# Loads of stage two issued from one queue, and the stage-one transpose in two instructions

## What is computed

```
adj = relu(einsum('bn,tnm->btm', x.reshape(b, n*d), masker_param) + masker_bias)   # b, t, 50, 50
adj = adj / (adj.sum(-1) + 1e-6)
m = einsum('btnm,btmd->btnd', adj, x @ weight)
r, z, ng = split(m @ w_ih.T + b_ih + x @ w_hh.T + b_hh, 3)
h = (1 - sigmoid(z)) * tanh(sigmoid(r) * ng) + sigmoid(z) * x
h = layernorm(batchnorm(h)); w = softmax(h @ attn_w.T + attn_b); out = einsum('btn,btnd->btd', w, h)
```

## Time and profile before

| what | value |
| --- | --- |
| median of 3 runs | 2257.29 us (2251.59 to 2257.75) |
| time of the profiled execution | 2254.87 us |
| its span, first to last instruction | 2253.1 us |
| PE busy | 2141.4 us (95%) |
| DVE, ACT, POOL busy | 1221.3, 866.1, 66.7 us |
| granted TensorE clock, mean | 0.971 |
| q1 (SP) and q10 (ACT) moved | 237.53 MB and 37.69 MB |

### The profile page before, as it was taken

How to read it: one execution, slowest core, us unless ns; L and a number is a source line. 1 busy time by engine, 2 the same in 40 slices (tenths; PEclk the granted TensorE clock), 3 DMA queues, 4 the chain that set the end, 5 groups by cost and what they waited for, 6 DMA issues and landing times. The chain is left out here.

```text
span 2253.1 us, 33249 instructions
## 1 busy us (share of the span) xinstructions
PE 2141.4 (95%) x11694; PEld 1680.5 (75%) x11694; DVE 1221.3 (54%) x2370; ACT 866.1 (38%) x1471; POOL 66.7 (3%) x68
## 2 busy tenths in 40 slices
PE   8999999999999999999999999998988988996898
PEld 7888888888888888888888887776766766775333
DVE  5444334444265443344443453776776766878667
ACT  4211111111033111111110123776876776875862
POOL 0000000000000000000000000100100110110000
PEclk9999999999999999999999999998999998998899
DMA  7321222221254212222202234675556566564660
GB/s 249 140 100 51 93 99 104 99 95 45 104 187 147 105 56 83 99 104 102 101 35 104 104 103 119 160 171 162 150 153 167 137 158 171 141 177 138 196 184 11
DMA packets 148058, 276.08 MB, mean 123 GB/s; under 512 B 11565, under 2 KB 106061, under 8 KB 143053
## 3 DMA queue, kind: packets, MB, share of 16 engines
q1 hardware_dynamic: 129836, 237.53, 34.7%
q10 hardware_dynamic: 18144, 37.69, 5.6%
HBM read 196.01 MB, written 79.17 MB: 122 GB/s over the span
## 5 line engine op out<-in xcount | busy, mean ns | idle before, releaser
L431 PE MATMUL psum<-w_hi,x_lo 128*128 128x500 f32 x2080 | 806.3, 388 | 8.2 <-DVE w_lo L289 8.2
L431 PE MATMUL psum<-w_lo,x_hi 128*128 128x500 f32 (+1 forms) x2080 | 807.8, 388 | 0.0
L431 PE MATMUL psum<-w_hi,x_hi 128*128 128x500 f32 x1920 | 743.2, 387 | 0.0
L340 DVE TENSOR_REDUCE rows<-u 128x10 f32<-128x500 f32 x160 | 107.7, 673 | 741.4 <-ACT u L302 741.3
L302 ACT ACTIVATE u<-psum 128x500 f32<-128x500 f32 x160 | 93.9, 587 | 1048.0 <-PE psum L431 1048.0
L431 PEld LDWEIGHTS psum<-w_hi,x_lo 128*128 128x128 f32 x2080 | 391.0, 188 | 88.8 <-issue 8.2
L431 PEld LDWEIGHTS psum<-w_lo,x_hi 128*128 128x128 f32 (+1 forms) x2080 | 390.8, 188 | 78.1
L431 PEld LDWEIGHTS psum<-w_hi,x_hi 128*128 128x128 f32 x1920 | 360.6, 188 | 72.3
L746 PE MATMUL psum<-adj_sb,xs_sb 100*64 100x100 f32 x2048 | 222.6, 375 | 4.4 <-PEq L148 4.4
L746 PEld LDWEIGHTS psum<-adj_sb,xs_sb 100*64 100x64 f32 x2048 | 154.7, 153 | 55.8 <-issue 39.4
L609 ACT ACTIVATE r_gate<-psum,bias 64x400 f32<-64x400 f32 x256 | 151.2, 591 | 60.5 <-PE psum L773 58.9
(11 more groups left out here) (168 smaller groups left out, 2103.9 us busy)
## 6 DMA issues: line engine op xcount, KB each, us to landing
w_raw<-W SPq DMA_DIRECT2D x140, 500.0 KB, 6.5
adjT<-at SPq DMA_DIRECT2D x160, 320.0 KB, 2.3
adj_sb<-adjT SPq DMA_DIRECT2D x32, 800.0 KB
xs_sb<-xz SPq DMA_DIRECT2D x16, 1600.0 KB
hF<-hC ACTq DMA_DIRECT2D x96, 256.0 KB, 2.9
h<-hF SPq DMA_DIRECT2D x64, 256.0 KB, 4.0
adj_sb<-adjT SPq DMA_DIRECT2D x32, 450.0 KB
xg_sb<-xg ACTq DMA_DIRECT2D x14, 800.0 KB, 17.3
```

The costliest lines, as they stand in the source:

```text
L340: nc.vector.tensor_reduce(rows[:, 0], u[:, c2], AX.X, ALU.add).then_inc(dve_step, 1)
L431: last = nc.tensor.matmul(mm_out(w % 2), a[0:r, w, k, :], b[0:r, k, :], start=k == 0 and n == 0, stop=k == KF and n == 1)
```

## The change

SP now issues all three loads of stage two. Its wait per tile is for `h_ready` (the last state of tile t) in place of `ax_done`, and `load_xg` stands ahead of `load_adj` and `load_xs`. `reload_xg` leaves ACT. In stage one `turn_squares` issues two transposes of 320 columns in place of one of 640; only the second signals.

```diff
--- before.py
+++ after.py
@@ -355,7 +355,8 @@
                     dve.wait_ge(an_cleared, 1)
                 else:
                     dve.wait_ge(at_stored[c2], 8 * (c - c2))
-                nc.vector.transpose(at[:, c2], an[:].rearrange("p n (k s) -> p k n s", s=TB)).then_inc(at_ready, 1)
+                nc.vector.transpose(at[:, c2, 0], an[:, :, 0:TB])
+                nc.vector.transpose(at[:, c2, 1], an[:, :, TB:2 * TB]).then_inc(at_ready, 1)
 
             def weight_blocks(dve):
 
@@ -533,7 +534,8 @@
                 for r in range(2):
                     tile = it * 2 + r
                     if more:
-                        sp.wait_ge(ax_done, (tile + 1) * ROUNDS)
+                        sp.wait_ge(h_ready, (tile + 1) * ROUNDS)
+                        load_xg(sp, shared, ins, tile + 2, r)
                         load_adj(sp, shared, adjT, tile + 2, r)
                         load_xs(sp, shared, ins, tile + 2, r)
 
@@ -559,11 +561,6 @@
         @block.scalar
         def _(act):
             act.wait_ge(bias_ready, 1)
-
-            def reload_xg(tile, r):
-
-                act.wait_ge(h_ready, (tile - 1) * ROUNDS)
-                load_xg(nc.scalar, shared, ins, tile, r)
 
             def x_hi(it, r, k):
 
@@ -619,8 +616,6 @@
                     nc.scalar.activation(n_bank(s), n_in[:, s % 2], ACT.Tanh).then_inc(n_ready, 1)
                     if q and (r or not (isinstance(it, int) and it == 0)):
                         store(it * 2 + r - 1, q - 1)
-                    if q == 0 and (r and more or not r and not (isinstance(it, int) and it == 0)):
-                        reload_xg(it * 2 + r + 1, 1 - r)
 
             nc.scalar.activation(r_gate[:, 0:1], bias[:, 0:1], ACT.Sigmoid).then_inc(warmed, 1)
             for k in range(XPARTS):
```

## The result

The changed kernel takes 2263.66 us (median of 20 runs) against 2255.35 us for the kernel before (20 runs beside it): a ratio of 1.0039, 95% interval 1.0030 to 1.0048. It is slower by 0.4%, some 9 us. The profiled execution of after took 2261.48 us, its span is 2259.5, its mean granted clock 0.972.

The account below looks back on a forecast made before the run. Stage one was taken as PE-bound, stage two as bound by no engine alone, with waits. Later loads (+34.3 us) and transposes (+0.2) made +34.5 on 2254.9: 2289 us, 1.4% slower, range 2275 to 2315.

Parts of the forecast that it names:

- The mechanism: Stage two: loads start 10.7 us later and land 7.2 us after PE gets there; PE waits in tiles 1 to 14.
- The length of the loads: Stage two, tiles 1 to 14: loads need 32.7 us, landing 32.8 us after the last state.
- the sign that this step is wrong: Stage two: SP's issue to PE's release under 31 or over 35 us would show the load step wrong.
- The other way to the number: Loads read from the middle of stage two: about 28 us, with xg_sb ahead 28.0 to 33.3; not the one taken.
- Were it all of the 800 KB, they would add nothing: Stage two: if q10's old stretch already held all of xg_sb, moving it ahead adds 0 us, otherwise up to 5.3.
- The release: Stage two: from PE's release to the tile's last state 12.2 us, taken from tile 0; at least 10.7 by tile 5.
- DVE's stop: DVE's 38.8 us in 5 stops at L644, after stage two's jump back; 48 more instructions can end or keep it.
- the forecast hardly hangs on it: Stage two: if DVE's stop stays, five tiles take 45.7 us, +3.5 us in all; if it goes, 45.0 holds.
- Rival 1: Stage two: loads of 30.0 us, release 10.7, DVE's stop gone; 40.8 us a tile, 2231 us; chance 0.09.
- Rival 2: Stage two: loads short but DVE's stop stays in five tiles; 2255 us, no change; chance 0.09.
- Rival 3: DVE's stop at stage two's jump grows by a second 7.7 us; +42 us on top, 2331 us; chance 0.08.
- Rival 4: Stage two: adjacency meets its point, so the change only removes 34.0 us of waits; 2221 us; chance 0.03.

Follow-up runs that it names:

- only the wait moved: Kernel before with two transposes, SP waiting for the last state before adj_sb and xs_sb, xg_sb still issued by ACT: 2242.7 us, ratio 0.9951.
- 64 memsets: Changed kernel with 64 one-column memsets of an unused buffer at the start of DVE's list: 2271.54 us, ratio 1.0083 to the kernel before.
- adjacency early: Changed kernel, but adj_sb issued after the last aggregation, xg_sb and xs_sb after the last state: 2166.97 us, ratio 0.9606 to the kernel before.
- one transpose: Changed kernel with its new loads, but one transpose of 640 columns again in stage one: 2266.45 us, ratio 1.0042 to the kernel before.
- memsets: Kernel before, one transpose and old loads, with 16 one-column memsets of an unused buffer at the start of DVE's list: 2232.23 us, ratio 0.9899.
- adjacency early, one transpose: Changed kernel with adj_sb after the last aggregation, xg_sb and xs_sb after the last state, and one transpose: 2223.89 us, ratio 0.9862 to the kernel before.
- the split: Kernel before with its old loads, only the transpose split into two of 320 columns: 2238.13 us, ratio 0.9918.

## Why the prediction was right or wrong

**The mechanism: right.** The loads wait for the last state, PE gets to its point before they are there, and the stop is 3.3 to 6.8 us in each of tiles 1 to 14, 65.5 us in all; I had said 6 to 8, about 100. The waits for `xg_sb` are gone and buy nothing, stage one is as long as before, and the transposes are hidden.

**The length of the loads: this step failed.** The prediction said 32.8 us from state to release, taken from stage two's start, and set aside the 28.0 to 33.3 of the middle of stage two as the worse way. Measured are 30.3, and from the issue 30.1, under the 31 that the prediction had named as the sign that this step is wrong. Over fourteen tiles that is 14 x 2.5 = 35 us too much. It is more than the forecast's whole excess over the measured spans (34.5 against 6.4, 28 us), because the release, below, was put too low.

The start is one sample, and of another state than the middle. Twelve of the traces have these same first loads, behind the identity's: from the issue of `xg_sb` to the full semaphore they take 30.6 to 33.3 us, mean 31.8, and before's 32.6 is the third longest. In tiles 1 to 14 of after the same stretch is 28.5 to 32.1 us, mean 30.0. So the sample was 0.7 us above its own mean, and that mean 1.8 us above the steady state. Why the start is longer is not known. Two causes lie near. In before, SP issues the next tile's adjacency while these loads still run:

```profile
1386.93 0.44 SPq L143 DMA_DIRECT2D xg_sb<-xg  x1
...
1416.27 2.08 SPq L131 DMA_DIRECT2D adj_sb<-adjT  x4
```

These are of the kernel before; the second issue is 3.3 us ahead of PE's release at 1419.59, and in after, where it comes only at 1430.98, the first loads take 31.3 us. But with only the wait moved, and in after with 64 memsets, it comes after 1432 as well, and they take 32.7 and 33.3. So the overlap does not explain it. The other is the identity's load: out of the way, they take 30.5, and with it 30.6 once (adjacency early). One run without it doesn't show its share.

The other way to the number would have done better. In before the adjacency of tiles 2 to 15 landed 28.1 to 31.4 us after its issue, mean 29.7, with the 800 KB of `xg_sb` beside it in q10; the 28 that I read came from a single stretch, the shortest of the fourteen. After has the same bytes in one queue, and 30.1 from the last state. "Were it all of the 800 KB, they would add nothing" was that case, and I had it as an end of the range. With only the wait moved and `xg_sb` in q10 it lands at 29.7. That the loads are 2.6 us shorter without `xg_sb` shows that the old stretch had paid for most of them already.

**The release: 12.9 us, not 12.2.** +0.7 a tile, +10 us. Tile 0, from which it was taken, has no tile before it to turn: PE's busy time by group in the 13.1 us from 1634.40 has a row that the same stretch of tile 0 lacks,

```profile
L785 PE MATMUL psum<-ident_sb,hT 128*128 128x128 f32 x5 | 1.4, 413 | 0.0
```

and PE is busy for 13.10 of these 13.10 us, so that these five lie on the path. They cost 1.4 us, of which tile 0's own lower clock (mean 0.76 in its stretch, 0.82 here) makes good a part. The clock also parts the tiles from one another: in tiles 4, 6, 9, 11 and 13 the release takes 12.3 to 12.4 us for the same products, with a mean clock of 0.86 to 0.87; in the others it takes 12.8 to 13.3, with 0.76 to 0.82.

**DVE's stop: went, as the prediction left open,** and "the forecast hardly hangs on it" holds: 1.0042 with it and 1.0039 without (one transpose). But I treated it only as something that the new loads cover, and not as what the change gives back. On the kernel before, its going is worth 18 us (0.8%, two transposes) to 23 us (1.0%, memsets). The change first wins these, and then loses some 27 by the loads, of which the later wait has some 7 and the move of `xg_sb` to the head of SP's queue 20.

**Stage two's start and stage three:** the last state of tile 0 ends 1.3 us earlier (1430.5), and stage three takes 188.0 us against 189.5. The transposes cost 0.14 us a window where 0.21 was estimated.

**The sum again with what was measured:** 14 x 43.2 = 604.8 less 595.7 is +9.1, less 1.3 and 1.5 is +6.3; the spans differ by 2259.5 - 2253.1 = 6.4 us.

**The rivals.** Rival 1 (loads 30.0, stop gone) had the load right within 0.3 us and the stop right, and fell by its release of 10.7 us: that was tile 5's, which has no wait and so no half clock. Rival 2 failed with the stop; its time of no change was the nearest of the five to what was measured. Rival 3 did not appear: even where the stop returns beside the new loads it lasts at most 4.8 us in one piece (one transpose) or 7.9 (64 memsets), and not 15. Rival 4, the adjacency in time, is false for this change: without `xg_sb` at all the adjacency still lands 27.6 us after the last state, behind the 25.6. Its 2221 us are near the 2223.9 of the kernel with the adjacency early and DVE's stop left in, but by luck: there the nine tiles without the stop are 39 us shorter than before, and the five with it 6 us longer. With the stop gone as well it is 2167.

**What stays open.** Why stage two's first loads take longer than the later ones is open, and so is the rule by which a place of DVE's loop stops (see the last section). Why the load part ranges from 28.9 to 32.4 us over the tiles of after is not explained. The longest, tile 14's, has stage three's first reads in the same queue (`h` from `hF`, issued from 2015.3 us on); the others were not looked into.

## What to carry to other kernels

Give each transfer the wait that its own buffer needs: here one late wait for three loads made the kernel 0.4% slower, and 1.2% slower than the kernel with the old loads and DVE's stop gone, and separate waits made it 3.9% faster. Take the length of a load from the middle of the steady state, over many turns, with what runs beside it there, and not from the one place that shows the same order. Before a change of a few instructions is judged, see whether a loop's code now lies elsewhere: a stop without a releaser at a jump, with its instruction packets, can be worth more than the edit.

## What the runs showed of the hardware

**The place of a loop's code decides whether it stops.** DVE's loop in stage two is 289 instructions. In the kernels whose loop lies where it lay before, or 112 instructions further on (the split and 64 memsets), q14 has 50 packets and DVE stops at each of the five jumps back, for up to 9.3 us; 16 or 48 further on it has 24 or 25 and there is no stop. The packets are 8192 B (0.20 MB in 24). With the stop, five of them are fetched in each turn of the loop (before, 1640 to 1726 us); without it none is fetched from 1545 to 2004 us (after), so that the loop's code stays at hand from its second turn on. Why these places and not those is not settled. The expectations of the two memset kernels counted blocks of 128 instructions, of which the loop covers four from one place and three from another; this count foretold both, and fits all four places, but four are few, and how much the engine holds was not measured. ACT's loop of 244 instructions (236 in after) never stopped.

The Trainium skill, in "Runtime: NRT & Kernel Launch", section "Instruction fetch mechanics", has a branch out of the code at hand wait for a fetch. The runs agree, and add the price: up to 9.3 us a jump, 10.6 us of the end where nothing hides it. The section also gives blocks of 256 instructions and 16 KiB, which is 64 B each, and two of them held at a time. DVE's packets here are half as large, and the trace of after has 20 of them from instruction 320 to 1470 of DVE's list (each loop counted once), about one for 60 instructions. Even if two packets make up one block of 16 KiB, only some 120 instructions of the trace go with it, so the 256 aren't borne out.

**A load behind a narrow one arrives in two parts.** Where `xg_sb` stands last, the trace has the 16 completions of one `xg_sb` as six, from 1548.8 to 1550.6 us, one at 1560.4, and nine from 1563.8 to 1566.1; tiles 2 to 15 all have them as six, one and nine. The load ahead of it, `xs_sb`, spans 100 partitions. The Trainium skill, in "DMA: Bandwidth & Descriptors", section "Why a DMA increments its semaphore by 16 and not by 1", has a transfer spread over the largest count of engines, up to 16, that divides the slowest dimension of both its sides, which for 100 partitions is 10. The six and ten agree with it: six engines are free early, and ten carry `xs_sb` first. The one and nine agree as well: two of the four adjacency DMAs have 18 rows (nodes 33 to 50), for which the rule gives 9 engines, so that one engine carries `xs_sb` but not these. No run loads `xs_sb` over 16 engines, so what that would bring is not known.

**Half clock after a short wait.** PE waited 4.82 us at 1634.40, and the granted clock was 1.00 just before, 0.50 (1.2 in place of 2.4 GHz) in 1634 to 1639. What this costs went by the number of stops and hardly by their length. PE's busy time in tiles 1 to 14, for the same products:

| kernel | PE's stops in these tiles | PE busy | more than without a stop, per stop |
| --- | --- | --- | --- |
| adjacency early | none | 510.1 us | |
| after, `xg_sb` not loaded | 14, of 0.7 to 3.1 us | 532.4 us | 1.6 us |
| adjacency early, one transpose | 5, of 8.1 to 8.7 us | 521.0 us | 2.2 us |
| after | 14, of 3.3 to 6.8 us | 539.4 us | 2.1 us |
| after, `xg_sb` last | 14, of 11.0 to 15.5 us | 543.7 us | 2.4 us |
